# Turning TensorE's step loop back between attention and the scores instead of after the scores

## What is computed

```python
x = x + L0(x)   # x W^T + s * (x A[b]^T) B[b]^T         one 512 x 512 matrix and a rank-16 adapter
x = x + L1(x)   # einsum('bct,bcd->bdt', x, w1[b])      mixes the 64 tokens of a sequence
x = x + L2(x)   # causal attention, 16 heads of 32: softmax(beta q k^T / sqrt(32)) v, then Wo
x = x + L3(x)   # einsum('bct,bcd->bdt', x, w3[b])      mixes tokens again
```

## Time and profile before

| what | value |
| --- | --- |
| median of three runs | 613.75 us |
| the profiled execution | 613.62 us |
| its span, first to last instruction | 611.9 us |
| granted TensorE clock, mean | 0.997 of full speed |
| TensorE matmuls busy | 603.4 us, 99% |
| VectorE, ScalarE, GpSimd busy | 64%, 37%, 18% |

### The profile page before, as it was taken

One profiled execution on the slowest core, in us unless ns is written; L12 is line 12 of the kernel. 1 busy time (PEld: TensorE's weight loads), 2 busy tenths in 40 slices (PEclk: granted clock), 3 DMA queues, 4 the chain that ended last, 5 costly groups with the idle time before them and its releaser, 6 DMA issues.

```text
span 611.9 us, 21509 instructions
## 1 busy us (share of the span) xinstructions
PE 603.4 (99%) x8534; PEld 521.6 (85%) x8534; DVE 392.5 (64%) x573; ACT 224.5 (37%) x434; POOL 109.9 (18%) x101
## 2 busy tenths in 40 slices
PE   9999999899999999999999999999999999999998
PEld 8798889788898988889788898988889898888885
DVE  4789865665657666575765657567575766647374
ACT  4545451342514334152442424344251443513222
POOL 2004030301303021040401204030030302103030
PEclk9999999899999999999999999999999999999999
DMA  9862323222222323223222322322222231210312
GB/s 297 163 135 58 84 61 77 75 61 74 63 72 77 92 65 71 73 58 79 73 64 73 79 73 65 88 73 60 74 63 73 74 82 54 66 70 4 71 41 104
DMA packets 65272, 48.29 MB, mean 79 GB/s; under 512 B 16922, under 2 KB 51738, under 8 KB 65242
## 3 DMA queue, kind: packets, MB, share of 16 engines
q1 hardware_dynamic: 60090, 42.63, 26.8%
q10 hardware_dynamic: 5152, 5.24, 3.0%
HBM read 30.54 MB, written 17.30 MB: 78 GB/s over the span
## 4 chain that ended last, share of the span: by engine, by line
PE 96%; DVE 2%; issue 1%; ACT 0%; DVEq 0%
PE banks L654 10%; PE banks L649 10%; PE banks L650 10%; PE banks L677 5%; PE banks L748 5%; PE banks L679 5%; PE banks L749 5%; PE banks L755 5%; PE banks L681 5%; PE banks L589 5%; PE banks L591 5%; PE banks L593 5%; PE banks L702 5%; PE banks L694 4%; PE banks L718 3%; PE banks L633 3%
## 5 line engine op out<-in xcount | busy, mean ns | idle before, releaser
L649 PE MATMUL banks<-x1T_hi,w_hi 128*128 128x256 f32 x512 | 129.8, 286 | 0.0
L650 PE MATMUL banks<-x1T_hi,w_lo 128*128 128x256 f32 x512 | 128.2, 283 | 0.0
L649 PEld LDWEIGHTS banks<-x1T_hi,w_hi 128*128 128x128 f32 x512 | 98.0, 191 | 0.5 <-ACT x1T_hi L914 0.2
L650 PEld LDWEIGHTS banks<-x1T_hi,w_lo 128*128 128x128 f32 x512 | 98.1, 192 | 0.0
L654 PE MATMUL banks<-x1T_lo,w_hi 128*128 128x256 f32 x512 | 82.4, 283 | 0.1
L1429 POOL TENSOR_TENSOR probs<-probs,row_max 128x1024 f32<-128x1024 f32 x32 | 61.0, 1905 | 115.4 <-DVE row_max L1209 115.4
L1411 POOL TENSOR_TENSOR w_own<-w_in,own 128x128 f32<-128x128 f32 x32 | 14.9, 466 | 362.5 <-PE banks L616 267.5
L654 PEld LDWEIGHTS banks<-x1T_lo,w_hi 128*128 128x128 f32 x512 | 70.6, 192 | 0.4 <-DVE x1T_lo L1120 0.3
L1195 DVE TENSOR_TENSOR qkT<-banks,beta 128x512 f32<-128x512 f32 x32 | 22.0, 689 | 60.4 <-PE banks L654 60.4
L914 ACT ACTIVATE x_y<-banks 128x512 f32<-128x512 f32 (+1 forms) x17 | 9.9, 585 | 128.8 <-PE banks L616 122.0
L1213 DVE TENSOR_REDUCE row_sum<-probs 128x16 f32<-128x1024 f32 x32 | 39.0, 1218 | 25.1 <-ACT probs L996 25.1
(11 more groups left out here) (138 smaller groups left out, 1057.3 us busy)
## 6 DMA issues: line engine op xcount, KB each, us to landing
x_rows<-x_in SPq DMA_DIRECT2D x64, 128.0 KB, 2.4
x_kept<-x_rows SPq DMA_DIRECT2D x16, 512.0 KB, 3.6
x_in<-in_x_dram SPq DMA_DIRECT2D x60, 128.0 KB, 2.8
out_dram<-x_y SPq DMA_DIRECT2D x15, 512.0 KB, 3.0
b_sel<-b_parts SPq DMA_DIRECT2D x180, 32.0 KB, 1.7
w_in<-in_L_cond_weights_dram SPq DMA_DIRECT2D x128, 16.0 KB
probsT<-in_L_cond_W_dram ACTq DMA_DIRECT2D x1, 1024.0 KB, 6.3
probs<-in_L_cond_Wk_dram ACTq DMA_DIRECT2D x1, 1024.0 KB, 6.0
```

What stands on the lines that cost most here:

```text
L649: nc.tensor.matmul(out_ap, w_hi[:, w, c, cols], x1T_hi[:, c, :], start=(c == 0), stop=False)
L650: nc.tensor.matmul(out_ap, w_lo[:, w, c, cols], x1T_hi[:, c, :], start=False, stop=False)
```

## The change

TensorE's `step(i)` now begins with `scores(i)`, where it ended with `scores(i + 1)`. The order of the matmuls from one step to the next is the same; what moves is the place at which one step ends and the next begins, and with it the place at which the hardware loop turns back. In step 13 (`LAST_ALIKE + 1`), the first behind the loop, `values(i, 0)` is put ahead of `scores(i)`. Its wait for `q_scaled` is there because both use bank OUT[0]. SyncE adds one to `y_copied_act` and `y_copied_dve` at the start, so that a wait inside the loop never compares with zero; all the waits on these two count one more.

```diff
@@ sync @@
+            sp.sem_inc(y_copied_act, 1)
+            sp.sem_inc(y_copied_dve, 1)
...
-                sp.wait_ge(y_copied_act, i + 1)
-                sp.wait_ge(y_copied_dve, i + 1)
+                sp.wait_ge(y_copied_act, i + 2)
+                sp.wait_ge(y_copied_dve, i + 2)
@@ tensor @@
             def scores(i):
+                if after(i, -1):
+                    pe.wait_ge(y_copied_act, i)
+                    pe.wait_ge(y_copied_dve, i)
                 for mm, k_copied in enumerate((k_copied_act, k_copied_dve)):
...
             def step(i):
                 prev, nxt, nxt2 = after(i, -1), after(i, 1), after(i, 2)
                 if not prev:
+                    scores(i)
                     pe.wait_ge(part_split, len(PARTS_V))
-                values(i, 0)
-                if prev:
+                    values(i, 0)
+                elif parted(i) and i == LAST_ALIKE + 1:
+
+                    pe.wait_ge(q_scaled, 2 * i + 1)
+                    values(i, 0)
+                    scores(i)
                     values(i, 1)
+                else:
+                    scores(i)
+                    for t in range(TILES):
+                        values(i, t)
...
                         attend()
-                if prev:
-                    pe.wait_ge(y_copied_act, i)
-                    pe.wait_ge(y_copied_dve, i)
-                else:
+                if not prev:
                     pe.wait_ge(part_split, len(PARTS_V) + len(PARTS_O))
-                scores(i + 1)
...
             adapters_down(1)
-            scores(0)
             in_steps(pe, step)
```

More of the change, by code:

```diff
@@ L495, in _ @@
             for t in range(TILES):
-                sp.wait_ge(y_copied_act, PAIRS + t)
+                sp.wait_ge(y_copied_act, PAIRS + 1 + t)
                 if t == 1:
-                    sp.wait_ge(y_copied_dve, PAIRS)
+                    sp.wait_ge(y_copied_dve, PAIRS + 1)
                 sp.dma_start(out_v[PAIRS - 1][:, t, :], y[:, t, :]).then_inc(y_stored, 16)
@@ L903, in _ @@
             pe.wait_ge(x2_added, TILES * PAIRS)
-            pe.wait_ge(y_copied_act, PAIRS - 1)
+            pe.wait_ge(y_copied_act, PAIRS)
             for n, to in enumerate((MIX[1], OUT[0])):
```

## The result

The changed kernel takes 616.24 us, the median of six runs (615.91 to 616.88), against 614.05 us for the kernel before (613.18 to 614.53, six runs). The medians are 2.19 us apart, 0.36%; the ratio on record is a little larger, 1.0043, its 95% interval 1.0031 to 1.0056. So the change makes the kernel slower by 2 us or a bit more. The profiled execution took 616.35 us.

A forecast was written before the change was run, and what follows sets the result against it. TensorE, 99% busy with matmuls, was taken to bound the kernel, so its pauses add to the time. Terms -3.6 + 3.3 + 1.7 = +1.4 on 613.62 gave 615.0 us; range 611.2 to 616.9, own range 614.2 to 616.0.

The forecast's parts named there:

- The first pass: First loop pass, attention to scores: the 1.60 us stall and the clock's fall behind it go, -3.6 us.
- The turn: Loop turn moved between attention and scores: 0.3 us more at each of eleven turns, +3.3 us.
- The balance: Net cost of one moved turn, new gap against old gaps: +0.26 us, taken as 0.3; bounds about nothing to 0.4.
- Entry and start: Ahead of the loop: the added semaphore increments on SyncE cost nothing, 0 us.
- The loop's end: Step 13, values before scores: mask 2.6 us later, TensorE waits for VectorE's copy before adapters_down's last pair, +1.7 us.
- the switch: Step 13, adapters_down: change between small and large matmuls, raising the 1.6 us wait to 1.7.
- The rule against the trace: Loop turns: the skill page's fetch at taken branches out of a two-page window is not borne out by eleven packet-free turns.
- A: Loop turn: nearly free, its three instructions run while attention's matmuls drain; about -1.8, 611.8 us; chance 0.24.
- D: Loop turn: balance of only 0.15 us, so the sum is 0, 613.6 us; chance 0.16.
- B: Loop's end: the clock falls after waits among small matmuls, 1.8 us more, 616.8 us; chance 0.11.
- C: Code late behind the loop, 617 us, or the first pass's stall stays, 618.6 us; chance 0.07.

The follow-up runs named there:

- e2_step1_out: The kernel before with step 1 written out ahead of the loop, which then starts at step 2; 616.59 us, ratio 1.0040.
- e6_turn_in_long: The kernel before with the loop's turn moved between the values and layer 0, matmul order unchanged; 611.38 us, ratio 0.9956, and 612.22 us, ratio 0.9970, when run again.
- e1_no_swap: The changed kernel without the special order in step 13, so scores come before both values again; 614.19 us, ratio 1.0006.

## Why the prediction was right, point by point

The forecast was 615.0 us on a sum of +1.4; the span moved by 2.7. The direction was right and each of the mechanisms is borne out, as far as the points below say. The term of the turn and that of the loop's end were too small, and all four terms missed to the same side, so the small sum came out at nearly twice its size.

- **The first pass, predicted -3.6, measured -3.46.** The stall went, the clock stayed at 1.00. `e2_step1_out` shows that TensorE stands still where attention and scores are both new code. That the code arrives too late is argued from the packet of the instruction queue beside the stall, and no run delayed a packet. The packet alone does not tell: the changed kernel has it too. In the kernel before it starts at 107.53 us and takes 0.98 us by the trace's record, and TensorE goes on at 109.83, so what fills the last 1.3 us is open. Within the term, the clock's part is 1.5 to 1.6 us rather than 1.8, and the rest 2.2 rather than 1.8, by `e6_turn_in_long`.
- **The turn, predicted +3.3, measured +4.1 (11 x 0.37).** The step that was mis-sized is "So the new gap is 0.22 + 3 x 0.1 = 0.52 us". The loads show 0.65 us, and 0.65 - 0.10 + 0.06 - 0.22 = 0.39 would have given 0.37 well. The missing 0.13 has two parts by the trace's records of the sequencer, in the turn at 144 us. From the register move to the first load it takes 0.42 us, where it takes 0.06 in the kernel before, so the three instructions add 0.37 us to the loads, 0.12 each and not 0.1; the runs without one and two of them agree (0.65, 0.51, 0.40). And the branch starts 0.04 us before attention's last load ends, where it starts 0.10 us before the scores' last load ends at 185.20, which makes 0.06. In the loop's distance an instruction counts for 0.08 to 0.09 us, three of them for some 0.26 of the 0.37 if the third is like the two, and no run takes the other 0.11 apart. The prediction went from 0.26 to 0.3 because "The matmuls pause slightly longer than their loads". At this place they pause less (0.47 against 0.65 us), so those 0.04 us brought the term nearer by luck. The balance lay within the bound that was stated, 0.4. The balance's other part was right: 0.16 us saved at the old place, 0.15 in `e6_turn_in_long`.
- **Entry and start, predicted 0, measured +0.11.** That is less than what the same stretch varies by between the profiled executions of unchanged code (105.6 to 106.8 us over all kernels here).
- **The loop's end, predicted +1.7, measured +1.96.** The mask came 2.67 us later (predicted 2.6) and the waits are 0.43 and 0.75 us (predicted 0.5 and 1.0); TensorE's busy time grew beside them, which the prediction had as the switch, at 0.1. The copy that gates `adapters_down` lands 17.43 us behind attention (528.14 - 510.71), predicted 17.45 (527.4 - 509.95). What was mis-sized is "From about 525.8 to 527.4 makes 1.6, with the switch 1.7": the last pair of `adapters_down` lies behind the copy. It starts 0.15 us after the copy and `layer1` 0.31 us after it, where 0.1 was allowed for both. `e1_no_swap` puts 1.76 of the 1.96 on the new order.
- **The rule against the trace.** The prediction says that the eleven turns show no packet of the instruction queue. The earlier trace rows begin at 116 us and cover the last ten; the first turn, at 110.7 us, has packets around it. The conclusion stands on the ten.
- **The rivals.** A (a turn nearly free, 36.4 us) and D (36.55) fall with 36.77. B falls with a granted clock of 1.00 over the whole span, despite the two waits. C falls with the 128 scores in one piece at the first turn, and with `e1_no_swap` at the loop's end.

The terms as measured, 0.11 - 3.46 + 4.07 + 1.96 = 2.7, are the whole difference of the spans. The time of 616.24 us lies above the forecast's own range (to 616.0) and within the range given (to 616.9).

**What stays open.** `e6_turn_in_long` is the fastest kernel here, and it keeps the stall of the first pass, 2.2 us with the clock at 1.00 and 3.7 with its fall. Whether attention and scores can be kept apart in the first pass while the turn lies among long matmuls wasn't tried.

## What to carry to other kernels

In a loop whose engine never idles, the place of the turn is worth choosing. Here the branch and its waits were hidden behind long matmuls, and behind small ones each sequencer instruction showed, times the number of turns. A stall that appears in the first pass alone is paid once. Before moving the turn to avoid it, multiply what the new place costs by the count of turns. When a chain of other engines is started later, look at every place where TensorE meets it, and count the work that stands between the awaited copy and the next stage, too.

## What the runs showed of the hardware

- A turn of the loop on TensorE costs 0.16 us between small and long matmuls, 0.15 us less than that among long ones (36.40 and 36.25 us a turn), and some 0.5 us between two stretches of small ones, with the waits that stand there (36.77).
- TensorE's taken branch lasts 208 ns in the median and 76 ns where the loop is left. The Trainium skill, "Advanced Engine Details and Errata", "Control Flow Timing", gives about 108 ns for a compare-and-branch; the trace has twice that when it is taken.
- After the same stall the clock does not always fall: the first profiled execution of `e6_turn_in_long` stands still for 1.87 us and keeps a granted clock of 1.00, the second for 1.80 us and has 0.84 in the window shown. In the first set of experiments the kernel before had a mean clock of 0.997 in 25 of its 29 runs and of 1.000 in four, which took 612.96 to 613.24 us. The median of the 25 is 614.33 us, but they spread from 613.05 to 614.87, so the times alone do not give the price of the fall; the 1.5 to 1.6 us above come from the traces.
